# One pool of eight PSUM banks for every stage of a six-stage transformer kernel, taken by the planned end of use

## The reference, cut to what matters

```python
x = x + 0.5 * ffn0(layernorm(x))    # silu(x Wg * sg) * (x Wu * su), then Wd * sd; 512 -> 1536 -> 512, weights rounded to fp8
x = x + attn0(layernorm(x))         # 16 query heads of 32, 4 kv heads, rope, biases, causal softmax
x = x + 0.5 * ffn0(layernorm(x))
x = x + 0.5 * ffn1(layernorm(x))    # silu(x Wg) * (x Wu), then Wd; 512 -> 2048 -> 512
x = x + attn1(layernorm(x))         # 16 heads of 32, causal softmax
x = x + 0.5 * ffn1(layernorm(x))
```

## Time and profile before

| | |
|---|---|
| median of 3 runs | 2771.48 us (2770.33 to 2771.82) |
| the profiled execution | 2772.28 us |
| its span | 2770.5 us |
| busy: PE / DVE / ACT / GpSimd | 95% / 48% / 39% / 23% of the span |
| mean granted TensorE clock | 0.991 |

### The profile page before, as it was taken

The page is one execution under the profiler, slowest core; times in us unless marked ns, Lnnn a source line. Parts: engine busy times, 40 slices in busy tenths (PEclk is TensorE's granted clock), DMA queues, the critical chain, the costliest instruction groups (busy, mean ns, idle before and its releaser), DMA issues.

```text
span 2770.5 us, 35782 instructions
## 1 busy us (share of the span) xinstructions
PE 2638.7 (95%) x13216; PEld 1996.1 (72%) x13216; DVE 1339.3 (48%) x2712; ACT 1085.3 (39%) x1994; POOL 637.9 (23%) x1105
## 2 busy tenths in 40 slices
PE   6999789998999999999999999999999999999999
PEld 4788655475557888888888887655865578888887
DVE  7777655555646444533333345554455453333333
ACT  7554345635564223411212133556355641112111
POOL 3333511331223234411111111223122331111110
PEclk9999989999999999999999999999999999999999
DMA  4222021111111110000000002231223200000001
GB/s 141 69 70 71 29 63 35 51 41 38 36 55 50 35 42 8 23 31 23 23 23 25 30 8 62 67 77 55 51 60 73 55 31 24 23 23 23 31 16 61
DMA packets 60654, 121.63 MB, mean 44 GB/s; under 512 B 11840, under 2 KB 12864, under 8 KB 60480
## 3 DMA queue, kind: packets, MB, share of 16 engines
q1 hardware_dynamic: 60480, 119.35, 15.1%
HBM read 63.73 MB, written 13.63 MB: 28 GB/s over the span
## 4 chain that ended last, share of the span: by engine, by line
PE 76%; DVE 5%; issue 4%; ACT 2%; SPq 2%; DMA 1%; POOL 1%; DVEq 0%; ACTq 0%; POOLq 0%
PE psum L752 58%; PE psum L872 7%; PE psum L837 6%; PE psum L854 4%; SPq L1433 1%; PE psum L761 1%; DVE s1a0masked L1239 1%; ACT s4a1e L1051 1%; DVE s4a1masked L1239 1%; DVE tmp L1211 1%; PE psum L892 1%; PE psum L844 0%; POOL x L1347 0%; ACT s1a0qs L1004 0%; DVE s4a1y L1265 0%
## 5 line engine op out<-in xcount | busy, mean ns | idle before, releaser
L752 PE MATMUL psum<-hA_hi,wmem 128*128 128x256 f32 (+1 forms) x1536 | 404.9, 337 | 9.5 <-DVE tmp L1211 5.0
L752 PEld LDWEIGHTS psum<-hA_hi,wmem 128*128 128x128 f32 x1536 | 269.2, 191 | 47.3 <-DVE s1a0negmax L1239 7.5
L752 PE MATMUL psum<-hA_lo,wmem 128*128 128x512 f32 (+1 forms) x864 | 293.7, 340 | 0.0
L1239 DVE CUSTOM_DVE_ANT_0 s4a1masked<-psum,mask_q 128x640 bf16<-128x640 f32 (+7 forms) x256 | 188.7, 755 | 142.1 <-PE psum L837 89.4
L1239 DVE CUSTOM_DVE_ANT_0 s1a0masked<-psum,mask_q 128x640 bf16<-128x640 f32 (+7 forms) x256 | 188.3, 755 | 127.3 <-PE psum L837 74.5
L1051 ACT ACTIVATE s1a0e<-psum,p_scale 128x384 f32<-128x384 f32 (+5 forms) x384 | 203.9, 589 | 111.5 <-PE psum L854 109.3
L1051 ACT ACTIVATE s4a1e<-psum,p_scale 128x384 f32<-128x384 f32 (+5 forms) x384 | 204.3, 589 | 91.7 <-PE psum L854 90.2
L1178 DVE SCALAR_TENSOR_TENSOR x<-psum,x 128x512 f32<-128x512 f32 x256 | 175.5, 688 | 86.3 <-PE psum L752 82.4
L1149 DVE TENSOR_TENSOR s5f1prod<-psum,s5f1silu 128x512 f32<-128x512 f32 x64 | 44.2, 691 | 298.8 <-PE psum L752 298.8
L1149 DVE TENSOR_TENSOR s3f1prod<-psum,s3f1silu 128x512 f32<-128x512 f32 x64 | 44.2, 691 | 294.1 <-PE psum L752 294.1
L752 PE MATMUL psum<-s3f1w,s3f1a 128*128 128x512 f32 x768 | 181.0, 391 | 0.9 <-POOL s3f1w L1337 0.9
(11 more groups left out here) (208 smaller groups left out, 5010.9 us busy)
## 6 DMA issues: line engine op xcount, KB each, us to landing
s1a0qst<-s1a0qs SPq DMA_DIRECT2D x96, 128.0 KB
s4a1qst<-s4a1qs SPq DMA_DIRECT2D x96, 128.0 KB
s4a1kst<-s4a1ks SPq DMA_DIRECT2D x96, 128.0 KB, 2.3
raw<-in_gate SPq DMA_DIRECT2D x44, 256.0 KB, 2.7
raw<-in_up SPq DMA_DIRECT2D x44, 256.0 KB, 2.7
raw<-in_down SPq DMA_DIRECT2D x44, 256.0 KB, 2.8
rounded<-s0f0w SPq DMA_DIRECT2D x24, 256.0 KB, 2.0
s2f0w<-rounded SPq DMA_DIRECT2D x24, 256.0 KB, 5.1
```

The source lines that it names most:

```text
L752: ins = pe.matmul(out_, w, m, start=n == 0, stop=n == len(terms) - 1)
L1239: dve.tensor_tensor_reduce(T[s]["masked"][b][turn % 2][:, 0:width].rearrange("p (z w) -> p z w", **bare), scores, mask_q[:, SEQ - width:SE ...
```

## The change

All eight banks are one pool for all steps. For each bank the list now keeps the place in the list of the step in which its content is read last (`EMPTIED_BY` names it where it is another step; for `pv` it is the head's `take`). A step takes the bank for which that place is earliest; a step that wants two takes the neighbouring two whose later place is earliest. Which earlier step PE waits for follows from that as before. The list of steps itself, and all else, stays.

```diff
@@ -358,37 +358,43 @@
         return self.place[step]
 
 
+BANKS = 8
+EMPTIED_BY = {"piece": "piece_out", "v_tile": "v_out", "v_turn": "v_out", "m_tp": "m_lo",
+              "y_turn": "y_fin", "ln_tp": "ln_lo"}
+
+
+def banks_wanted(step):
+
+    kind = step[0]
+    if kind == "gu":
+        return 2
+    if kind == "row":
+        return 1 + ((step[-1] + 1) * P > CH)
+    if kind == "pv":
+        return int(step[-1] == 0)
+    return int(kind in ("key", "down", "ln_tp", "piece", "v_tile", "v_chunk", "v_turn", "m_tp",
+                        "y_turn", "y_tp", "oproj"))
+
+
 def bank_turns(plan):
 
-    banks, earlier, used = {}, {}, {}
-    slots, accs, acc_at = list(range(6)), [6, 7], 0
-    for step in plan:
-        kind = step[0]
-        width = 0
-        if kind in ("gu",) or kind == "row" and (step[4] + 1) * P > CH:
-            width = 2
-        elif kind in ("ln_tp", "piece", "v_tile", "v_chunk", "v_turn", "row", "m_tp", "key",
-                      "y_turn", "y_tp") or kind == "down" and step[4] >= 2:
-            width = 1
-        if width:
-            age = {bank: n for n, bank in enumerate(slots)}
-            first = min(range(6 - width + 1),
-                        key=lambda i: max(age[j] for j in range(i, i + width)))
-            mine = list(range(first, first + width))
-            for bank in mine:
-                slots.remove(bank)
-                slots.append(bank)
-        elif kind in ("down", "oproj") or kind == "pv" and step[4] == 0:
-            mine = [accs[acc_at % 2]]
-            acc_at += 1
+    at = {step: now for now, step in enumerate(plan)}
+    banks, earlier, used, empty = {}, {}, {}, [-1] * BANKS
+    for now, step in enumerate(plan):
+        width = banks_wanted(step)
+        if not width:
+            continue
+        first = min(range(BANKS - width + 1), key=lambda i: max(empty[i:i + width]))
+        mine = list(range(first, first + width))
+        banks[step] = mine
+        earlier[step] = [(used[bank], banks[used[bank]].index(bank)) for bank in mine
+                         if bank in used]
+        if step[0] == "pv":
+            then = at[("take",) + step[1:-1]]
         else:
-            continue
-        banks[step] = mine
-        earlier[step] = [(used[bank], k) for bank, k in
-                         ((b, used.get(b) and banks[used[b]].index(b)) for b in mine)
-                         if bank in used]
+            then = at[(EMPTIED_BY.get(step[0], step[0]),) + step[1:]]
         for bank in mine:
-            used[bank] = step
+            used[bank], empty[bank] = step, then
     return banks, earlier
```

## The result

The changed kernel takes **2734.51 us** (median of 4 runs, 2729.72 to 2735.06) against 2770.9 (4 runs, 2770.29 to 2771.82) for the kernel before beside it: ratio 0.9865, interval 0.9847 to 0.9882. It is 36.4 us faster; 2726.5 was forecast, a gain of 45. The profiled execution of the changed kernel is the fastest of its four: span 2728.0 against 2770.5, so the traces differ by 42.5 us. Over all runs on record single executions of the changed kernel took 2729.7 to 2736.6 us and those of the kernel before 2769.4 to 2775.8, so the one scatters about as much as the other; one more execution of the kernel before, 3273.61 us at a granted clock of 0.752, was in a slow state and is left out.

What follows compares the result with a forecast made beforehand. PE, busy 95%, was taken as the bound, with 95 us lost to bank waits. Direct gain 79 less 19 (scarce pairs), 5 (wait instructions) and 10 (reader lag) gave 45 us: 2726.5 us against the median, range 2702 to 2762.

Steps and rivals of the forecast that it cites:

- Item 3: Attention, `y_turn` banks: 33 `row` steps wait for `y_fin`, about 18 us; the new order gains 17 us.
- item 2: Attention, `m_tp` banks: `row` 5 no longer waits for `m_lo`, though 17 take the pair `row` 4 left; gain 15 us.
- item 1: Attention: two accumulator banks join the pool, so rows and keys turn through seven banks, not six; no separate gain given.
- Item 5: Other bank waits, such as projections behind `tmp`, `negmax`, `qs`, keys behind keys, first `y_turn`: 34 of 36 us gone.
- Item 6: Attention: neighbouring bank pairs are scarce, so rows and keys wait behind rows on them; 19 us lost, bounds 0 and 28.
- rival C: Attention: rows 5 and 6 queue for the previous row's pair in all 64 heads; 18 us slower, 2790; chance 0.04.
- Item 7: PE, mostly `pv` for `exp`: 110 more second waits at 0.05 us each cost 5 us, bounds 1 and 11.
- Item 8: Attention: readings by DVE, and ACT, move forward less than PE does; 10 us lost, bounds 0 and 45.
- Item 9: Key 0 of a head waits for two `mrow` DMAs when PE is early; costed at nothing, 64 us at very most.
- A: Rival: readers lag in attention, 40 us lost to DVE and ACT lag, 15 us gained, 2757; chance 0.20.
- B: Rival: all bank waiting goes, 95 us gained, 2677; chance 0.07.
- D: Rival: no change, PE's real bound is its issue between `pv` steps and gaps only move; 2766 to 2777; chance 0.05.

Runs made afterwards that it cites:

- The eight-bank run: Changed kernel with all eight banks in one pool, but a bank's age counted from when it was given, as before: 2751.07 us, 0.9922.
- the table: Changed kernel with each step's bank read from a searched table that keeps steps, above all rows, off banks read late: 2731.34 us, 0.9848.
- the later split: Changed kernel with one unit more between the load of a q, k or o attention weight and its split: 2726.06 us, 0.9837.

## Why the prediction was right, point by point

**Direction, size and place** were right: 36.4 us by medians and 42.5 by the traces for 45; 25.7 for 25 in the first attention stage, 14.5 for 17 in the second, 2.4 for 3 in feed-forward. The marks named in advance came out: `mrow` and `y` gone for the row steps, `negmax` up from 10.1 to 12.7 and in both stages, more weight loads of L872 behind ACT's `e` (21.7 us for 9.0). The size, though, owes something to luck, as the items show. None of the marks for a wrong forecast did: rows behind `negmax` are far from 60 us, PE's busy share rose, and L878 and L860 show 9.7 us for `e` together.

**What bounds the kernel** (95 us in banks): 99 by the later count, 39 left. The correction of the idle shown by the tails was needed; the 56 us of the rows by themselves, less items 6 to 8, would have left only 22.

**Items 1 to 4** (accumulators, `m_tp`, `y_turn`, `row` behind `row`): the waits they name went as told. Item 3 was priced too high. The case of the earlier trace rows and the same head after:

```profile
1792.83 1.38 PE L872 MATMUL psum<-s4a1e,s4a1v 128*33 128x384 f32 x8
...
1763.68 1.38 PE L878 MATMUL psum<-s4a1e,s4a1v 128*33 128x384 f32 x8
1764.99 0.67 PE L843 MATMUL psum<-s4a1kst,s4a1qst 128*128 128x448 f32 x2
```

From the first `pv` matmul to `row` 6 it was 1794.49 - 1792.83 = 1.66 us and is 1.31: the wait cost 0.35, of which 0.28 was shown, and not 0.46. Behind a `pv` step the tail hides 0.07 us, behind the `m_tp` cases of item 2 it hides 0.2 (25.7 us by starts for 19.5 shown). The 33 steps of item 3 cost 10.5 us by their starts, not 18. As all banks together cost 96 to 99, what item 3 has too much is missing in the rest. The eight-bank run shows that item 2 hangs on the order and not on item 1: with eight banks and the old age the `mrow` waits stay at 22 us.

**Item 5 was too large.** Of its 34 us, about 8 stood before a step whose input was late anyway. The first `v_turn` of the attention stage started at 346.23 us before, after 8.36 us of waiting, and at 344.57 after, behind 16.26 us. Its projections no longer wait for a bank, but `tmp` comes when ACT has made it. ACT in turn goes at the pace of DVE, which clears the stacks between the projections' pieces (three `MEMSET` of 0.91 us in front of each of several `tmp`, before and after the change); no run moved these. The step failed where it took the waits of L752 behind `tmp` as won, without asking what the next step but one waits for; "L822 stays" was read off the list of waits, where it had to grow.

**Item 6 was right in the waits and wrong in the price.** It left 95 - 79 + 19 = 35 us of bank waiting, and 39 are counted. Where `row` 5 follows `row` 4 with only a key and a transpose between, all 26 wait, 0.66 to 0.77 us, as taken. Of the 17 `row` 6 behind `row` 5, one waits, 0.31 us, so the upper bound and rival C had these too high. But the table that takes nearly all waits of the rows away gains 3.7 us: the forecast charged them as if nothing stood behind. With the later split the same table is worth 2726.06 - 2714.73 = 11.3 us.

**Item 7 was wrong**: 5 us for 110 waits (the program grew by 104 instructions); by the run with 512 more waits it is some 0.3, and with the scatter about 1 at most. The later starts of keys with two waits, from which I took the price, have another cause, which I did not look for.

**Item 8**, the lag of DVE (10 us), was not measured by itself: shortening its readings wins 13.9, but part of that is item 6's waits. So 6 and 8 are not separate costs, and were added as if they were: 79 less the 7.9 of item 5 and the 5.3 at DMAs (item 9) is 66, and 66 - 42.5 = 23 us remain for items 6 to 8, where the forecast had 34. That makes up for what items 5 and 9 lacked, and this is the luck in the number: two errors of 11 and 13 us that cancel. Against the median's 36.4 the cancelling is less good, and the forecast is 8.6 us too high.

**Item 9 was too small.** The `mrow` DMAs, costed at nothing, show 5.1 us (3.7 in the second trace) where the earlier trace rows have 1.6. The place is the second sequence's head 1, in this stretch of the changed kernel's timeline:

```profile
606.67 0.60 SPq L1443 DMA_DIRECT2D s1a0qst<-s1a0kst  x1
606.97 0.27 DVE L1256 TENSOR_TENSOR s1a0mrow<-psum,s1a0mrow 8x128 fp32r<-8x128 f32 x1
607.31 1.78 SPq L1439 DMA_DIRECT2D s1a0kst<-s1a0ks  x3
609.13 1.39 SPq L1453 DMA_DIRECT2D s1a0qst<-s1a0mrow  x2
...
611.78 1.19 PE L860 MATMUL psum<-s1a0qst,s1a0kst 128*128 128x512 f32 x2 [3.82 <-DMA s1a0qst<-s1a0mrow]
```

`mrow` is written at 607.24, but SP is still issuing the stacking DMAs of the group and comes to it at 609.13. Before, that queue ran dry at 625.74, in time. The prediction looked at a head without stacking in front; PE's lead over the kernel before was 19.3 us at this head's `m_tp` and is 16.4 at the next head's, 2.9 given back. In the second trace PE came later, with a lead of 15.6, and gave back 0.5.

**Item 10** (feed-forward 0): f1 moved by 0.04 us at most.

**The rivals.** A (2757) had the right mechanism at a third of its price: 40 us for item 8, where an early reader gives back 13.9. B (all waiting gone) is refuted: all eight banks are in use, and 39 of 99 us of bank waiting stayed. C would have needed 1.5 us of new bank waiting per head; 39/64 = 0.6 is all that is there. D is refuted by the intervals.

In sum: 60 us of waiting went, and 42.5 came out. Of the 17.5 between, 7.9 are at `v_turn`, 3.5 at the `mrow` DMAs and 1.8 at the second attention's `kst` DMA (5.0 for 3.2); the last 4 I ascribe to steps that now meet their input sooner: PE's rows show `pv` behind `e` at 7.6 us for 2.7 before, and `oproj` behind `yT` at 2.8 for 1.4. In the second trace 20 us lie between, with 6.4, 2.1 and 2.2 at the three places and 5.7 at these two, so that some 3 are left. This account adds up rows of waits, which can hide one another; no run shows it as a whole. What stays open is why the second attention stage takes 533.0 us in one trace of the changed kernel and 535.4 in the other, while the first repeats to 0.1.

## What to carry to other kernels

A wait that is taken away is worth at most the distance to the next thing that its step, or the step behind it, would wait for; look for that before adding it to the sum, in the queue of the DMA issuer too. Two edits that each free one of two late parties can give more together than apart (20.3 against 12.7 us), so an edit that wins little should be tried again when the next bound is gone. With a pool of PSUM banks, the number and the order of reuse are two levers: here 22 us for two banks more, 11 for taking the bank that is read soonest, 38 for both. And the tail that hides a wait depends on the step before: take it from starts of the same pair of steps, held and not held, and not from one case.

## What was not expected of the hardware

A semaphore wait that is already met costs PE next to nothing between the matmuls of this kernel: 512 of them (335 more instructions in the trace) made 1 us, within the scatter. And 26.7 of 42.5 us came out of PE's busy time, with the same matmuls at nearly the same clock (0.991 and 0.992): in this profile, busy time holds waiting, 0.2 us where a `row` 5 is held behind transposes and 0.07 where a `row` 6 is held behind a `pv`.
